# Expert weights in two pieces: up weights and biases issued behind the last gelu, down weights behind the down projection

## The reference

```python
# layer 0: one expert a token, hidden width 1024
for e in range(8):
    h = gelu(x_flat @ w1[e] + b1[e])
    y = h @ w2[e] + b2[e]
    out = out + where(expert_idx == e, expert_w, 0.0)[:, None] * y
# layer 2: the two best of eight experts, hidden width 512
h = gelu(einsum('bsd,edh->besh', x, W1) + b1)
out = einsum('besh,ehd->besd', h, W2) + b2
y = einsum('bse,besd->bsd', gates, out)
```

## Time and profile before

| | before |
|---|---|
| runs, median of 3 (lowest, highest) | 1923.51 us (1921.05, 1930.52) |
| the profiled execution | 1912.75 us |
| its span | 1910.8 us |
| mean granted TensorE clock | 0.925 |
| TensorE matmul / weight load busy | 84% / 64% |
| VectorE, ScalarE, GpSimd busy | 56%, 47%, 20% |
| DMA | 152.23 MB, mean 80 GB/s |

### The profile page before, as it was taken

The page is one execution under the profiler, slowest core; times in us unless marked ns, Lnnn a source line. Parts: engine busy times, 40 slices in busy tenths (PEclk is TensorE's granted clock), DMA queues, the critical chain, the costliest instruction groups (busy, mean ns, idle before and its releaser), DMA issues.

```text
span 1910.8 us, 27535 instructions
## 1 busy us (share of the span) xinstructions
PE 1613.5 (84%) x10002; PEld 1224.3 (64%) x10002; DVE 1070.6 (56%) x3026; ACT 892.1 (47%) x2006; POOL 373.9 (20%) x469
## 2 busy tenths in 40 slices
PE   6999854999759999999858799999998679983666
PEld 5677654888646667666536667767766668872534
DVE  6767641222166666666567665555554534226787
ACT  3888811222227666666539355555543012222256
POOL 1000012111132333333240100000001422223644
PEclk8999967999979999999978899999997789996879
DMA  9000036776510000000000200000000448983001
GB/s 329 2 2 1 2 102 230 265 279 251 187 67 12 7 6 7 7 1 1 1 1 1 78 12 6 6 7 6 1 1 12 147 156 259 303 291 98 1 12 34
DMA packets 52694, 152.23 MB, mean 80 GB/s; under 512 B 7968, under 2 KB 38704, under 8 KB 44272
## 3 DMA queue, kind: packets, MB, share of 16 engines
q1 hardware_dynamic: 45168, 133.90, 20.7%
q0 software_dynamic: 5280, 14.47, 2.0%
q10 hardware_dynamic: 2112, 2.10, 0.3%
HBM read 133.89 MB, written 24.75 MB: 83 GB/s over the span
## 4 chain that ended last, share of the span: by engine, by line
PE 62%; DVE 15%; DMA 8%; POOL 5%; ACT 5%; issue 4%; POOLq 1%; SPq 0%; DVEq 0%; ACTq 0%
PE bank L1311 8%; PE bank L1365 6%; PE bank L1378 6%; PE bank L929 6%; PE bank L885 5%; PE bank L1352 5%; PE bank L1315 5%; DMA WB<-in_L0pack 3%; PE bank L1295 3%; PE bank L626 3%; POOL sorted_h L1103 2%; DMA WB<-in_L2pack 2%; PE bank L1714 2%; PE bank L642 2%; PE bank L282 1%
## 5 line engine op out<-in xcount | busy, mean ns | idle before, releaser
L1562 DVE TENSOR_REDUCE small<-bank 128x1 f32<-128x512 f32 x128 | 82.5, 686 | 108.7 <-PE bank L1365 108.7
L948 ACT ACTIVATE e2a<-bank,WB 128x128 f32<-128x128 f32 x156 | 44.5, 368 | 196.5 <-PE bank L929 196.5
L1558 DVE CUSTOM_DVE_ANT_0 p1f<-bank,p1f 128x512 f32<-128x512 f32 x128 | 83.2, 687 | 81.0 <-PE bank L1365 81.0
L1436 ACT ACTIVATE p2f<-bank,small 128x512 f32<-128x512 f32 x128 | 86.8, 683 | 86.2 <-DVE small L1562 86.2
L700 ACT ACTIVATE l<-l,small 128x256 f32<-128x256 f32 x256 | 108.9, 502 | 32.5 <-DVE small L767 32.2
L1433 ACT ACTIVATE p1f<-p1f,small 128x512 f32<-128x512 f32 x128 | 91.2, 713 | 67.5 <-DVE small L1558 67.2
L358 POOL TENSOR_SCALAR rs<-mv 128x4 f32<-128x4 f32 x20 | 4.7, 235 | 580.7 <-DVEq L230 550.0
L948 ACT ACTIVATE e0a<-bank,WB 128x128 f32<-128x128 f32 x128 | 36.5, 368 | 133.1 <-PE bank L929 133.1
L767 DVE CUSTOM_DVE_ANT_0 l<-bank,small 128x256 f32<-128x256 f32 x256 | 90.8, 420 | 13.2 <-PE bank L642 12.3
L1311 PE MATMUL bank<-WA,HT 128*128 128x256 f32 x384 | 93.9, 388 | 5.0 <-DVE p1f L1503 5.0
L1447 ACT ACTIVATE p2f<-bank 128x512 f32<-128x512 f32 x128 | 75.1, 598 | 40.6 <-PE bank L1352 39.0
(11 more groups left out here) (385 smaller groups left out, 3938.5 us busy)
## 6 DMA issues: line engine op xcount, KB each, us to landing
WB<-in_L2pack SPq DMA_DIRECT2D x39, 1026.0 KB, 7.9
WB<-in_L0pack SPq DMA_DIRECT2D x16, 2052.0 KB, 8.7
e0a<-in_L0pack SPq DMA_DIRECT2D x7, 2052.0 KB, 8.3
sorted_h<-in_blank SPq DMA_DIRECT2D x6, 1032.0 KB, 16.3
e2a<-sorted_h SPq DMA_DIRECT2D x39, 129.0 KB, 5.7
e2a<-given_y SPq DMA_DIRECT2D x8, 512.0 KB, 7.5
e0a<-sorted_h SPq DMA_DIRECT2D x23, 129.0 KB, 3.9
WB<-in_ctx ACTq DMA_DIRECT2D x4, 512.0 KB, 8.7
```

The source lines that it names most:

```text
L1436: ins = a.e.activation(P, k.bank(x), ACT.Exp, bias=self.mx[:, m:m + 1], accum_out=self.sm[:, m:m + 1])
```

## The change

A block's weights are loaded by two transfers with a semaphore each. The packed row is laid out as up weights, biases, down weights. The first piece (up weights and biases, `n1` = 2 ff + nf words) waits until the last gelu of block i - nwb is done, since then nothing reads the old one; the second waits for the down projection of block i - nwb, as the whole load did. TensorE waits for the first at the up projection and for the second at the down projection. In SP's loop iteration i issues the first piece of block i + nwb, the second piece of block i + nwb - 1 and the tokens of block i + 4; before it issued the tokens of block i + 5 and then the weights of block i + nwb. The bytes loaded are the same.

```diff
-        self.nw = 4 * ff + nf
+        self.n1 = 2 * ff + nf
...
-        self.aw = [k.dma(f"ew{i}", len(range(i, nt, nwb))) for i in range(nwb)]
+        self.a1 = [k.dma(f"ew{i}", len(range(i, nt, nwb))) for i in range(nwb)]
+        self.a2 = [k.dma(f"gather{4 + i}", len(range(i, nt, nwb))) for i in range(nwb)]
...
+            t.wait_ge(self.a2[i % self.nwb], i // self.nwb + 1)
             for c in range(nf):
                 t.wait_ge(self.gel, i * nf + c + 1)
-                ins = t.e.matmul(y[:, 0:256], self.gb[i % 2][:, c, :], w[:, 2 * self.ff + c * 256:2 * self.ff + (c + 1) * 256],
+                ins = t.e.matmul(y[:, 0:256], self.gb[i % 2][:, c, :], w[:, self.n1 + c * 256:self.n1 + (c + 1) * 256],
                                  start=c == 0, stop=c == nf - 1)
...
-        t.wait_ge(self.aw[i % self.nwb], i // self.nwb + 1)
+        t.wait_ge(self.a1[i % self.nwb], i // self.nwb + 1)
...
-                                   bias=w[:, 4 * self.ff + ft:4 * self.ff + ft + 1]).then_inc(self.gel.sem, 1)
+                                   bias=w[:, 2 * self.ff + ft:2 * self.ff + ft + 1]).then_inc(self.gel.sem, 1)
...
-    def load_w(self, s, i):
+    def load_up(self, s, i):
+
         w = self.w[i % self.nwb]
         s.wait_ge(self.routing, self.KNOWN)
+        s.wait_ge(self.gel, (i - self.nwb + 1) * self.nf)
+        x = s.e.value_load(self.ex[0:1, i:i + 1], min_val=0, max_val=7)
+        s.e.dma_start(w[:, 0:self.n1].rearrange("p (o n) -> p o n", o=1),
+                      self.pack[bass.ds(x, 1), :, 0:self.n1].rearrange("o p n -> p o n")).then_inc(self.a1[i % self.nwb].sem, 16)
+
+    def load_down(self, s, i):
+
+        w, n = self.w[i % self.nwb], self.n1 + 2 * self.ff
         s.wait_ge(self.dn, i - self.nwb + 1)
         x = s.e.value_load(self.ex[0:1, i:i + 1], min_val=0, max_val=7)
-        s.e.dma_start(w[:, 0:self.nw].rearrange("p (o n) -> p o n", o=1),
-                      self.pack[bass.ds(x, 1), :, :].rearrange("o p n -> p o n")).then_inc(self.aw[i % self.nwb].sem, 16)
+        s.e.dma_start(w[:, self.n1:n].rearrange("p (o n) -> p o n", o=1),
+                      self.pack[bass.ds(x, 1), :, self.n1:n].rearrange("o p n -> p o n")).then_inc(self.a2[i % self.nwb].sem, 16)
...
         for i in range(self.nwb):
-            self.load_w(s, i)
-        for i in range(5):
+            self.load_up(s, i)
+            self.load_down(s, i)
+        for i in range(4):
             self.load_x(s, i)
         for i in range(self.nt):
-            if i + 5 < self.nt:
-                self.load_x(s, i + 5)
             if i + self.nwb < self.nt:
-                self.load_w(s, i + self.nwb)
+                self.load_up(s, i + self.nwb)
+            if 0 < i and i - 1 + self.nwb < self.nt:
+                self.load_down(s, i - 1 + self.nwb)
+            if i + 4 < self.nt:
+                self.load_x(s, i + 4)
```

More of the change, by code:

```diff
@@ L2502, in pack @@
         return np.concatenate([w1.reshape(8, 2, 128, -1).transpose(0, 2, 1, 3).reshape(8, 128, -1),
-                               w2.reshape(8, -1, 128, 256).transpose(0, 2, 1, 3).reshape(8, 128, -1),
-                               b1.reshape(8, -1, 128).transpose(0, 2, 1)], axis=2)
+                               b1.reshape(8, -1, 128).transpose(0, 2, 1),
+                               w2.reshape(8, -1, 128, 256).transpose(0, 2, 1, 3).reshape(8, 128, -1)], axis=2)
     cols = np.concatenate([
```

## The result

| | before | changed |
|---|---|---|
| runs (median; lowest to highest) | 1922.43 us (1921.05 to 1930.52, 4 runs) | 1893.74 us (1887.41 to 1894.9, 4 runs) |
| ratio, 95% interval | | 0.9834 (0.9811 to 0.9857) |
| profiled execution / span | 1912.75 / 1910.8 us | 1887.41 / 1885.6 us |
| mean granted clock | 0.925 | 0.922 |
| e0 loop, first up projection to last down | 200.5 us | 183.8 us |

The change gains 28.7 us by the medians and 25.3 by the profiled executions.

The account below looks back on a forecast made before the run. It took the expert loops to be bound by the latency of one whole weight transfer. Gains of 15.2 us (e0) and 8.5 us (e2) summed to 23.7 us, from 1923.51 to 1899.8 us, range 1894 to 1913.

Parts of the forecast that it names:

- e0: First expert loop, 23 blocks, three weight buffers: 11.7 us of idle and 3.5 more come back, together 15.2 us.
- The bound: Up projections in both expert loops wait on one whole transfer: e0 lead 8.2 us against 0.7 and 8.5 to land.
- the ceiling of each: Most the loops can gain: e0 15.2 us, all expected; second expert loop (e2, 39 blocks) 11.3 us, 8.5 expected.
- the token load: In e2 tokens leave behind both pieces with a margin of 3.3 us, the tightest; 2.8 us of waits expected.
- Three signs of being right: e2: L914 waits 1 to 4 us for tokens, loop 6 to 10 us shorter, last 60 us DMA share above 0.93.
- the DMA work of a block in e2: Loads 3.67 us plus scatter 0.33 make 4.00 us a block in e2, against 3.74 us blocks without bias.
- 4.10: e2's DMA work a block in us, with 0.10 for the added transfers; range 4.00 to 4.45.
- the lower end of my bounds: Cost of added packets, from rows streamed alone: one row more costs next to nothing.
- My upper bound of 50 ns: Cost of one added packet, from comparing e0 and e2 loads; 0.45 us a block.
- A: Rival: in e2 the wait only moves to tokens at L914, leaving e0's 15.2 us; 1908.3 us, chance 0.20.
- B: Rival: each transfer holds SP's load queue in e2 for a fixed time, at worst 1.9 us; 1952.5 us, chance 0.05.
- C: Rival: loops end sooner, but the scatter DVE waits for or a lower clock takes it; 1923.5 us, chance 0.09.

Follow-up runs that it names:

- more_bytes_e2: Changed kernel with one more load of 256 KB a block in e2, into a place nobody reads; 1889.27 us, ratio 0.9845 against the kernel before.
- pieces_one_wait: Kernel before with weights in two pieces, both issued behind the down projection, tokens ahead, the up projection waiting for both; 1910.38 us against 1920.1, ratio 0.9958.
- four_pieces: Changed kernel with each piece cut in two halves, four transfers a block; 1885.2 us, ratio 0.9832 against the kernel before.
- both_again: Changed kernel timed again without an edit; 1889.6 us against 1918.18 for the kernel before, ratio 0.9847.
- pieces_both_late: Changed kernel, but both pieces wait for the down projection of block i - nwb, tokens ahead, separate TensorE waits kept; 1889.31 us, ratio 0.9852 against the kernel before.
- changed_third: Changed kernel timed once more without an edit; 1896.84 us against 1929.08 for the kernel before, ratio 0.9846.
- halves_by_partition: Kernel before, but a block's weights come in two loads of 64 partitions, the up projection waiting for both; 2028.39 us against 1929.08, ratio 1.0512.

## Why the prediction was wrong

**What held.** The bound (the latency of one whole transfer against a lead of one or two blocks), the two places, the ceiling of each. e0: 15.2 us forecast, 16.7 measured; the rest of it is five more up projections whose weights came just in time, with no idle shown and still 3.84 us, some 0.3 us each. e2's ceiling: 11.3 us forecast, 13.6 measured in the first profile with its 2 us of clock, and 10.1 to 11.7 in the runs that entered the loop like the kernel before. The new waits at L887 and for the gelu cost nothing, SP's issues cost nothing, and the token load is the first to be late when the engines do fill up. Three signs of being right did not come: L914 (now L916) waited 0 us for tokens and not 1 to 4, e2's loop lost more than 6 to 10 us, and the DMA share of the last 60 us was 0.86 and not above 0.93, because the last loads had landed before its end.

**The step that failed** is the DMA work of a block in e2, 4.00 us, and the 4.10 built on it. The term was to be "17 x (4.10 - 3.74) = 6.1 us" of backlog and 2.8 us of token waits; the token waits were 0. With 1.314 MB and the 390 GB/s of more_bytes_e2 the work is 3.37 us, below the block's 3.74, so no backlog can grow. The 4.00 came from busy share times time by blocks, which takes the share as a fixed cost of the bytes. It isn't: at a full share 4.00 us a block would be 328 GB/s, and the changed kernel moved 285 GB/s at 0.86 (1594 to 1614 us), 354 at 1.00 forty microseconds later, and more_bytes_e2 390 at 1.02. Durations of single packets in the DMA records show what stretches the share (ns, kernel before, 1645 to 1705 and 360 to 480 us):

```
bytes    count   median   90th percentile   mean
 1032     3528       47        47            51
 4096      868      159       159           160
 8208     1797      311       523           379
16416     1695      612      1102           719
```

The medians grow with the bytes and leave some 9 ns a packet (159 less 4096 B at the 301 ns that the step from 8208 to 16416 B costs for 8208 B), the lower end of my bounds. The means of the long ones lie a fifth above. In e0, behind the first packet of a load they were 1317 ns in the first half microsecond, 1019 and 724 in the next two, and 613 to 668 from then on; in e2 the mean was highest, 528 ns, one microsecond behind the first packet. The busy share counts such slow stretches as work. In e2 one engine gets 8 rows of weights, 8 of tokens and 2 of 4096 B from the scatter in a block: by the medians that is 3.2 us with the semaphore writes, by the means 3.8, an estimate from the table. My upper bound of 50 ns rested on the same reading.

That one term took 2.8 us off the forecast. Without it the sum is 26.5, the gain at which my own range for the forecast ended. I had put the range's low end at that ceiling and the spread of the runs, 1894, and the median fell 0.3 us below it. (Summed exactly, the ends are 1923.5 - 26.5 - 2.5 = 1894.5 and, with A, 1908.3 + 7.0 = 1915.3, and not 1894 and 1913.) The ceiling was taken as the best case, and it was too low: it put at nothing e0's 1.4 us of weights just in time, and the comparisons of the changed kernel with the one before, 1.53 to 1.66% or 29 to 32 us, all lie above it. By how little the range was missed is luck: the median of the kernel before was 1922.43 in this comparison and 1923.51 in the one that the forecast was carried from.

**The rivals.** A would have needed 4.6 us of work a block and is excluded by the 3.37. B is excluded by pieces_one_wait. The fit of 2.0 us a transfer that spoke for it is stated in the Trainium skill (DMA: Bandwidth & Descriptors, Anatomy of one DMA) for transfers issued by GpSimd, and the loads here are issued by SP. The Trainium skill (DMA: Bandwidth & Descriptors, Measured) advises loads of 1 MiB and more; here that does not bear out: in e2, every run that loaded the weights in half megabytes by columns, and the one in quarters, had a shorter loop (166.8 to 172.8 us) than the kernel before (180.5). By that page's other rule (Why small descriptors are slow), that overhead per packet matters only up to 256 B, the sum would have been a gain of 25.4. four_pieces agrees with the rule, its 18 more packets cost nothing; the gain of 28.7 is above the 25.4, in part because the 4.00 us in that sum were too much as well. C: the loops' gain arrived in the end. The 4.8 us between the loops in the first profile (1038.3 against 1033.5) were 1.3 us in both_again and 0.6 in pieces_both_late. In that profile TensorE was busy 926.9 us between the loops against 919.5, at a granted clock of 0.93 against 0.94, and idle 2.5 us less; it paused 5.1 and 3.5 us ahead of e2, and the 8.4 us wait for the first tokens of e2 was missing. The changed code does not run there. In changed_third that stretch took 1046.9 us, on a chip where the kernel before is 7 us slower as well. What sets the clock and these pauses isn't settled.

## What to carry to other kernels

When an engine waits for a transfer whose landing is as long as the lead, look first at whether all of it is needed at the first use: cutting it by the order of use and waiting for each part apart can bring all of the gain, with nothing issued earlier, as pieces_both_late shows. Don't take DMA busy share times time for the work of the bytes: take the rate of a stretch that is really full, or add a known load and see when something gives. If the ceiling of a gain is all that a loop can lose, ask what else could come back before making it the end of a range.

## What the runs showed of the hardware

- In e2 two transfers of half the columns land sooner than one of all: 5.0 and 5.5 us, issued 1.1 apart, against 7.9 (pieces_one_wait). In e0 they don't: 5.5 and 7.3 us, issued 1.1 apart, against 8.4. Halved rows in one transfer did not change the kernel's time (1.0009).
- Two transfers of 64 partitions each are slow: packets of 8208 B took 574 ns at the median against 311 (halves_by_partition, 1700 to 1800 us), and 242 GB/s filled the engines, where loads of 128 partitions reached 390 (more_bytes_e2).
- A packet took 9 ns and 36.7 ns for each 1000 B at the median, from 1032 to 16416 B, and some twice that at the start of a load in e0 (16416 B: 1317 ns against 612).
- The busy share isn't proportional to the bytes: 0.86 at 285 GB/s, 1.00 at 354, 1.02 at 390.
